# A post-norm attention and mixture-of-experts block on one core: reciprocals turned and spread by DMA, squares by one load, the output projection accumulated, and the swaps issued by ScalarE

## The reference

```python
# attention: 16 heads of 64, rotary embedding on interleaved pairs, causal
q, k, v = x @ Wq, x @ Wk, x @ Wv           # (128, 1024) each, split into heads
q, k = apply_rope(q), apply_rope(k)
attn = softmax(causal(q @ k.T / 8))
x = layernorm(x + (attn @ v) @ Wo + bo)
# mixture: 8 experts of 512, the best 2 of a softmax gate, renormalised
sparse_w = top2(softmax(x @ gate_w.T + expert_bias))
out = sum_e sparse_w[e] * (gelu(x @ w_up[e].T) @ w_down[e].T)
x = layernorm(x + layernorm(out) + x)      # the inner norm is the block's own
```

## Time and profile before

| | us |
|---|---|
| median of 3 runs | 805.34 |
| lowest and highest of them | 800.24, 806.1 |
| the profiled execution | 798.51 |
| its span, first to last instruction | 796.7 |

### The profile page before, as it was taken

How to read it: one execution, slowest core, us unless ns; L and a number is a source line. 1 busy time by engine, 2 the same in 40 slices (tenths; PEclk the granted TensorE clock), 3 DMA queues, 4 the chain that set the end, 5 groups by cost and what they waited for, 6 DMA issues and landing times.

```text
span 796.7 us, 20539 instructions
## 1 busy us (share of the span) xinstructions
PE 755.9 (95%) x5763; PEld 535.0 (67%) x5763; DVE 667.4 (84%) x2514; ACT 592.2 (74%) x1678; POOL 572.0 (72%) x701
## 2 busy tenths in 40 slices
PE   8899999999999999999999989999998899999995
PEld 4455666666666566666666656666656579999995
DVE  6688888999899879998999899989987974235997
ACT  3688878878878777877887768777877756565677
POOL 3686767558765877677768886976786266989983
PEclk9999999999999999999999999999999999999998
DMA  4576666456755566556555655565557667434525
GB/s 152 188 224 200 214 203 201 165 191 197 227 180 174 174 200 195 188 180 210 175 186 191 194 173 186 186 199 173 177 179 225 222 193 207 109 85 125 163 90 163
DMA packets 110719, 144.66 MB, mean 182 GB/s; under 512 B 13392, under 2 KB 86352, under 8 KB 110608
## 3 DMA queue, kind: packets, MB, share of 16 engines
q1 hardware_dynamic: 106240, 134.49, 53.8%
q0 software_dynamic: 4224, 8.72, 3.3%
q10 hardware_dynamic: 144, 0.13, 0.1%
HBM read 61.42 MB, written 45.17 MB: 134 GB/s over the span
## 4 chain that ended last, share of the span: by engine, by line
PE 67%; POOL 13%; DVE 8%; issue 7%; DMA 3%; ACT 1%; SPq 0%; DVEq 0%; POOLq 0%; ACTq 0%
PE AO L1109 15%; PE S_all L1068 14%; PE TB L1089 9%; PE AO L1129 5%; PE S_all L1256 4%; POOL yrows L956 4%; PE TB L1269 2%; POOL shared L973 2%; PE AO L1269 2%; DVE Sm L1609 2%; DMA qk<-shared 2%; DVE x_acc L1630 1%; PE TB L1000 1%; POOL shared L722 1%; PE TB L998 1%
## 5 line engine op out<-in xcount | busy, mean ns | idle before, releaser
L1376 ACT ACTIVATE Pr_all<-Sm,nmax 128x512 f32<-128x512 f32 (+3 forms) x512 | 281.8, 563 | 23.7 <-DVE nmax L1609 22.9
L1609 DVE CUSTOM_DVE_ANT_0 Sm<-S_all,causal 128x512 f32<-128x512 f32 (+3 forms) x512 | 223.0, 482 | 46.0 <-PE S_all L1068 45.9
L1068 PE MATMUL S_all<-qk 64*128 64x512 f32 (+3 forms) x1024 | 169.8, 446 | 10.9 <-DVE nmax L1609 8.6
L717 POOL TENSOR_TENSOR qk<-shared,qk 128x512 f32<-128x512 f32 x64 | 81.9, 1280 | 129.6 <-DMA qk<-shared 119.9
L1109 PE MATMUL AO<-PT,shared 128*64 128x128 f32 x1008 | 149.6, 438 | 13.1 <-issue 12.7
L1386 ACT ACTIVATE PT<-TB 128x768 f32<-128x768 f32 x189 | 107.8, 605 | 61.2 <-PE TB L1089 61.2
L1630 DVE SCALAR_TENSOR_TENSOR x_acc<-AO,rinv,x_acc 128x128 f32<-128x128 f32 x504 | 141.7, 344 | 3.5 <-POOL x_acc L769 1.3
L1068 PEld LDWEIGHTS S_all<-qk 64*128 64x128 f32 x1024 | 79.7, 187 | 82.6 <-issue 56.9
L1089 PE MATMUL TB<-ident,Pr_all 128*128 128x128 f32 x764 | 109.2, 279 | 3.6 <-ACT PT L1386 3.1
L1089 PEld LDWEIGHTS TB<-ident,Pr_all 128*128 128x128 f32 x764 | 82.0, 141 | 44.4 <-issue 40.6
L1109 PEld LDWEIGHTS AO<-PT,shared 128*64 128x64 f32 x1008 | 66.5, 136 | 61.1 <-issue 30.9
(11 more groups left out here) (335 smaller groups left out, 1459.0 us busy)
## 6 DMA issues: line engine op xcount, KB each, us to landing
turns<-turned_pr SPq DMA_DIRECT2D x63, 512.0 KB
PT<-turns SPq DMA_DIRECT2D x252, 128.0 KB
qk<-shared SPq DMA_DIRECT2D x124, 256.0 KB
wo<-in_wo SPq DMA_DIRECT2D x64, 64.0 KB, 3.1
PT<-yrows SPq DMA_DIRECT2D x7, 512.0 KB, 4.3
w_tile<-in_wup SPq DMA_DIRECT2D x10, 256.0 KB, 3.5
xt<-xrows SPq DMA_DIRECT2D x32, 65.0 KB, 2.7
x_acc<-in_x SPq DMA_DIRECT2D x8, 256.0 KB, 3.4
```

Of the source, the lines that this page charges most:

```text
L717: nc.gpsimd.tensor_tensor(qT[p][:, :], q_cos, qT[p][:, :], ALU.add).then_inc(q_ready, 1)
L1068: nc.tensor.matmul(SB[2 * (group % 2) + h][:, at:at + (qb + 1) * P], qT[p][half, qb * P:qb * P + P], kT[p][half, 0:(qb + 1) * P], start=Tr ...
L1376: nc.scalar.activation(Pr[j][:, 0:n], Sm[j], ACT.Exp, bias=nmax[:, j:j + 1], scale=-1.0, accum_out=rsum[p][:, h * QB + qb:h * QB + qb + 1] ...
L1609: nc.vector.tensor_tensor_reduce(out=Sm[j], in0=SB[2 * (group % 2) + h][:, at:at + n], in1=causal[:, T - n:T], scale=-0.125, scalar=HUGE, ...
```

## The change

1. **Reciprocals** (`invert`, `spread_norms`, `norm_o`): DVE inverts the row sums of unit u-1 at the head of iteration u and transposes them in squares of 32. SP writes them to a DRAM buffer `norms` (128 pieces of 128 bytes), waits for their landing, and reads them back spread over 128 partitions, 512 values in each, into a buffer: two rows of 2 KB, each repeated for 64 partitions. DVE multiplies the attention's output with them as it takes it from PSUM to OT (`norm_o`), in the place of ScalarE's `copy_o` and of DVE's `scale_y`, which stays for the last unit alone.
2. **Projection**: with OT already divided, `project_out` needs four products of 128 rows in the place of eight of 64, and accumulates over the 8 pairs of a sequence in one PSUM bank; DVE adds the bank to `x_acc` once a sequence (`add_y`). Wo is loaded in the first eight units and then kept.
3. **Squares by one load**: `store_turned` writes the rows in another order, so that one DMA of 512 KB can read back what four read before.
4. **Scores in one run**: group 2 has banks of its own (TB), and DVE masks all three groups without `scale_y` between them; the transposes of group 1 go to the score banks. `project_out` follows score group 2.
5. **Swaps**: ScalarE issues the two DMAs of `swap(u+1)`, between the last `exp` of unit u-1 and the first of unit u.

SP's order in an iteration is now: `spread_norms(u-1)` (store, wait, spread), `store_turned(u)`, wait, `load_turned(u)`.

```diff
-LOADED = LANES * 16
+LOADED = 16
...
+        def spread_of(u):
+
+            if u < PAIRS:
+                e = E - 2 + u % 2
+                return wdown[:, e * IB:e * IB + IB, :].rearrange("p a c -> p (a c)")
+            return hT[u % 2][:, :]
...
+        rinv, rinv_turned = (st2[:, i, :, :].rearrange("p n s -> p (n s)")[:, 0:SQ] for i in range(2))
...
-        def y_bank(u):
-            return (SB[2], SB[3]) if u == UNITS - 1 else (AB, OB)
+        y_bank, last_y = OB, (SB[2], SB[3])
 
         def turn_banks(u, group):
 
-            two = TB if u < UNITS - 1 or group == 0 else S_all[:, 2 * group - 2:2 * group, :]
+            two = S_all[:, 0:2, :] if group == 1 else S_all[:, 2:4, :] if group == 2 and u == UNITS - 1 else TB
             return two.rearrange("k b n -> k (b n)")
+
+        def score_bank(group, h):
+            return TB[:, h, :] if group == 2 else SB[2 * group + h]
+
+        def wo_of(u):
+
+            if u < PAIRS or u % PAIRS >= 6:
+                return wo[u % 2][:, :]
+            return w_tile[u % PAIRS // 4][:, u % 4 * P:u % 4 * P + P]
...
                 if first:
                     load_x(0)
+                elif u <= PAIRS:
+                    load_wo(u - 1)
+                if not first:
+                    spread_norms(u - 1, 1 - p)
+                if not last:
+                    store_turned(u, p)
+                    load_turned(u, p)
...
-                if not last:
-                    store_turned(u, p)
-                if first:
-                    load_turned(u, p)
...
+            def spread_norms(u, p):
+
+                sp.wait_ge(inverted, 2 * u + 2)
+                wait(sp, norms_in, 16 * (u - 1))
+                sp.dma_start(norms[p * SQ:p * SQ + SQ, :].rearrange("c (a r) -> a c r", r=SQ), rinv_turned).then_inc(norms_stored, 16)
+                sp.wait_ge(norms_stored, 16 * (u + 1))
+                wait(sp, norms_in, 16 * u)
+                wait(sp, o_ready, u - 1)
+                if u == PAIRS:
+                    sp.wait_ge(q_proj, PAIRS)
+                    sp.wait_ge(k_proj, PAIRS)
+                    sp.wait_ge(w_split, PAIRS // 2)
+                heads = norms[p * SQ:p * SQ + BLK, :].rearrange("(h q) t -> h (q t)", h=2)
+                sp.dma_start(spread_of(u), heads.unsqueeze(1).to_broadcast([2, D, T])).then_inc(norms_in, 16)
+
             def store_turned(u, p):
 
                 sp.wait_ge(turned, 2 * u + 2)
                 wait(sp, turns_in, LOADED * (u - 1))
-                sp.dma_start(turns[p * P:p * P + P, :], turned_pr[:, :, :, :].rearrange("p b c s -> p (b c s)")).then_inc(stored, 16)
+                sp.dma_start(turns[p * P:p * P + P, :].rearrange("(r a) n -> a r n", a=LANES),
+                             turned_pr[:, :, :, :].rearrange("p b c s -> p (b c s)")).then_inc(stored, 16)
 
             def load_turned(u, p):
 
                 sp.wait_ge(stored, 16 * (u + 1))
+                wait(sp, turns_in, LOADED * u)
                 wait(sp, pv_done, u - 1)
-                squares = turns[p * P:p * P + P, :].rearrange("(a r) (b n) -> b r a n", r=SQ, b=LANES)
-                for b in range(LANES):
-                    sp.dma_start(PT[p][SQ * b:SQ * b + SQ, LANES * (QB - 1):, :, :].rearrange("k a c s -> k a (c s)"),
-                                 squares[b]).then_inc(turns_in, 16)
-
-            def swap(u, p):
-
-                sp.wait_ge(k_read, u + 1)
-                sp.wait_ge(q_read, u + 1)
-                wait(sp, scored, BLK * (u - 1))
-                sp.dma_start(qk[p][0:P:2, :, :], qk_rot[1:P:2, :, :]).then_inc(swapped, 16)
-                sp.dma_start(qk[p][1:P:2, :, :], qk_rot[0:P:2, :, :]).then_inc(swapped, 16)
+                squares = turns[p * P:p * P + P, :].rearrange("(r a) (b n) -> b (r a) n", a=LANES, b=LANES)
+                sp.dma_start(PT[p][:, LANES * (QB - 1):, :, :].rearrange("k a c s -> k (a c s)"), squares).then_inc(turns_in, 16)
...
             def project_q(u, n, batch):
                 inputs_ready(n, batch)
-                if u == 2:
-                    pe.wait_ge(v_ready, 2)
-                elif u > 2:
-                    pe.wait_ge(pt_ready, 2 * (u - 3) + 1)
+                if u >= 2:
+                    pe.wait_ge(maxed, BLK * (u - 1))
...
             def transpose(u, p, group):
                 pe.wait_ge(exped, BLK * u + DONE_BY[group])
-                if u == UNITS - 1 and group > 0:
+                if u == UNITS - 1:
                     pe.wait_ge(maxed, BLK * UNITS)
+                    pe.wait_ge(pt_ready, 2 * u)
                 elif group == 2:
 
-                    pe.wait_ge(pt_ready, 2 * u + 1)
+                    pe.wait_ge(maxed, BLK * (u + 2))
                 else:
-                    wait(pe, pt_ready, 2 * u)
-                    pe.wait_ge(q_read, min(u + 3, UNITS))
-                    if u == 0:
-                        pe.wait_ge(k_read, 2)
+                    pe.wait_ge(maxed, BLK * (u + 1) + DONE_BY[0])
...
+                for i in range(QB):
+                    last = nc.tensor.matmul(y_bank[:, i * P:i * P + P], OT[p][:, i * P:i * P + P], wo_of(u),
+                                            start=(first and i == 0), stop=last_pair, skip_group_check=True)
+                last.then_inc(y_done, 1)
...
-                wait(pe, maxed, BLK * u)
+                wait(pe, maxed, BLK * (u - 1) + DONE_BY[1])
+                wait(pe, pt_ready, 2 * (u - 2) + 1)
                 score(u, p, 0)
-                if u >= 2:
...
+                    pe.wait_ge(maxed, BLK * u)
+                    wait(pe, pt_ready, 2 * (u - 1))
+                    pe.wait_ge(q_read, min(u + 2, UNITS))
                 score(u, p, 2)
+                if u >= 2:
+                    project_out(u - 2, p)
...
-                if u >= 2:
-                    copy_o(u - 2, p)
                 if not first:
                     for j in range(FIRST_OF[2], BLK):
                         exp(u - 1, 1 - p, j)
+                if 2 <= u < UNITS - 1:
+                    swap(u + 1, 1 - p)
...
+            def swap(u, p):
+
+                act.wait_ge(k_read, u + 1)
+                act.wait_ge(q_read, u + 1)
+                act.wait_ge(scored, BLK * (u - 1))
+                nc.scalar.dma_start(qk[p][0:P:2, :, :], qk_rot[1:P:2, :, :]).then_inc(swapped, 16)
+                nc.scalar.dma_start(qk[p][1:P:2, :, :], qk_rot[0:P:2, :, :]).then_inc(swapped, 16)
...
             def invert(u, p):
 
                 dve.wait_ge(exped, BLK * (u + 1))
-                wait(dve, y_read, 2 * u)
-                nc.vector.reciprocal(rinv[:, :], rsum[p][:, :]).then_inc(inverted, 1)
+                nc.vector.reciprocal(rinv[:, 0:BLK], rsum[p][:, :]).then_inc(inverted, 1)
+                if u < UNITS - 1:
+                    dve.wait_ge(inverted, 2 * u + 1)
+                    wait(dve, norms_stored, 16 * u)
+                    nc.vector.transpose(rinv_turned, rinv).then_inc(inverted, 1)
+
+            def norm_o(u, p):
+
+                dve.wait_ge(pv_done, u + 1)
+                dve.wait_ge(norms_in, 16 * (u + 1))
+                wait(dve, y_done, u - 1)
+                nc.vector.tensor_tensor(OT[p][:, :], o_bank(u), spread_of(u), ALU.mult).then_inc(o_ready, 1)
+
+            def add_y(b):
+
+                dve.wait_ge(y_done, min(PAIRS * (b + 1), UNITS - 1))
+                dve.wait_ge(x_set, b + 1)
+                rows = x_acc[:, b * QB:b * QB + QB, :].rearrange("p a c -> p (a c)")
+                nc.vector.tensor_tensor(rows, y_bank, rows, ALU.add).then_inc(y_read, 1)
...
+                if u >= 2:
+                    norm_o(u - 2, p)
+                if not first:
+                    invert(u - 1, 1 - p)
```

More of the change, by code:

```diff
@@ L22 @@
 BLK = 2 * QB
+Y_READS = B + 2
 ORDER = [(0, 3), (1, 3), (0, 2), (1, 2), (0, 0), (1, 0), (0, 1), (1, 1)]
@@ L142, with build_block @@
 HUGE = 3.0e38
-def build_block(nc, xT_h, x_h, wqk_h, wv_h, wo_h, bo_h, cos_h, sin_h, gate_h, ebias_h, wup_h, wdown_h, xrows, yrows, turns, out_h):
+def build_block(nc, xT_h, x_h, wqk_h, wv_h, wo_h, bo_h, cos_h, sin_h, gate_h, ebias_h, wup_h, wdown_h, xrows, yrows, turns, norms, out_h):
     ctx = ExitStack()
@@ L370, in build_block @@
         o_ready = sem("o_ready")
+        norms_stored, norms_in = sem("norms_stored"), sem("norms_in")
         y_done = sem("y_done")
@@ L400, in build_block @@
         y_in = [sem(f"y_in{i}") for i in range(B - 1)]
-        y_last_in = [sem(f"y_last_in{i}") for i in range(QB)]
+        y_last_in = [sem(f"y_last_in{i}") for i in range(len(PARTS))]
         summed, last_summed, spaced = sem("summed"), sem("last_summed"), sem("spaced")
@@ L545, in _, with load_wo, keep_wo @@
             rows, experts = [], []
+            def load_wo(u):
+                wait(sp, y_done, u - 1)
+                sp.dma_start(wo[u % 2][:, :], wo_h[bass.ds((u % PAIRS) * P, P), :]).then_inc(wo_in[u % 2], 16)
+            def keep_wo():
+                rows = wo_h.rearrange("(n p) c -> p n c", p=P)
```

(36 more changed lines are left out.)

105 lines of the change are left out of this document (54 added, 51 removed).

## The result

The changed kernel takes 1812.0 us (median of 4 runs, 1806.2 to 1817.8) against 803.1 us (4 runs, 800.2 to 806.1): 2.256 times the time before, 95% interval 2.243 to 2.269. The forecast was 1560 us, with a range up to 1800.

The account below looks back on a forecast made before the run. Few DMA engines on store, load and spread were to bound each unit through SP's chain, 22 us instead of 9.79; 62 x (22 - 9.79) = 757 us on 796.7, with 1.8 around it 1556, gave 1560 us, range 1240 to 1800.

Parts of the forecast that it names:

- The signs that the forecast named: DMA share below 0.5, two SP landing waits of 5 us or more, store at about 100 GB/s, stores 22 us apart.
- the sum of SP's chain: SP's queue per unit: spread 5.9, store 5.2, latency 1.3, load 6.6, small store 0.8, latency 1.3, issues 0.5: 21.6 us.
- load 131 / 19.8 = 6.6 us: Single load of the turned group: a quarter, 131 thousand bytes, per engine in 1 KB pieces, 6.6 us a unit.
- 5.9: Spread of the reciprocals: half of it on each of two engines in 2 KB pieces, 5.9 us a unit.
- 131 / 25.3 = 5.2 us: Store of the turned group: a quarter, 131 thousand bytes, per engine in 4 KB pieces, 5.2 us a unit.
- 26 us and 1800 us: Unit and kernel time if latencies double and swaps and small store fall fully into SP's chain.
- The waits between score group 2 and the masks go: Attention unit: these waits disappear, worth at most 0.6 us a unit.
- DVE's lighter unit: DVE loses eight instructions and gains a multiplication and a small transpose: 1.9 us less a unit.
- the first rival: All sixteen engines work on every transfer; units at 9.3 us, about 775 us, faster; chance 0.12.
- All sixteen engines: Every DMA transfer uses all sixteen engines, so PE runs closed up: about 775 us; chance 0.12.
- ACT holds the swap: Sixteen engines, but swaps wait for the last exp on ACT; POOL's loop 10.3 us, 830 us; chance 0.03.
- Only the spread is narrow: Other transfers re-cut over sixteen engines; SP's chain 12.4 us a unit, 960 us; chance 0.03.

Follow-up runs that it names:

- r_k8: o_wide_sp with the 64 repeats of each spread transfer's source written as 8 x 8 (outermost count 8): the spread moves for 2.6 us (median).
- r_k2: o_wide_sp with the 64 repeats of each spread transfer's source written as 2 x 32 (outermost count 2): the spread moves for 7.3 us (median).
- w_load: Changed kernel with only the load cut into four transfers of 32 partitions: 1443.0 us, a unit of 19.8.
- w_store: Changed kernel with only the store cut into four transfers of 32 rows, new row order kept: 1450.9 us, a unit of 19.9.
- b_one_load: Kernel before with only the store's new row order and the single load of 512 KB: 1237.8 us, a unit of 16.6.
- a_tiny: Changed kernel with swaps of 16 of the 512 columns: 1696.7 us, a unit of 23.7.
- w_spread: Changed kernel with only the spread cut into one transfer per head, outermost count 64: 1690.1 us, a unit of 23.7.
- n_sp: Changed kernel with old store and four loads, swaps issued by SP, small store and spread left out, norm_o multiplying by the cosine table: 795.8 us, ratio 0.986.
- o_wide: Changed kernel with the store and four loads of before, and the spread cut by heads into two transfers: 878.1 us, ratio 1.092.
- o_wide_sp: o_wide with SP issuing the swaps between the store and the loads, as before: 859.5 us, ratio 1.067.
- o_act: o_wide_sp with the small store and the spread issued by ScalarE at two places of its unit: 834.7 us, ratio 1.038.
- n_act: n_sp with the swaps issued by ScalarE: 811.5 us, ratio 1.005.
- o_squares: Changed kernel with the row order and four loads of before put back, the spread staying narrow: 1207.1 us, unit 16.1.

## Why the prediction was right in its mechanism and short in its size

**The mechanism held.** Transfers with outermost counts of 4, 4 and 2 run on that few engines: `r_k8` to `r_k2` show it for one dimension alone, `w_load`, `w_store` and `b_one_load` for the load and the store. The signs that the forecast named came: a DMA share of 0.28 with two grown waits of SP, DVE waiting 624.3 us for the spread, busy shares of PE and DVE near half and a third. Two came in another size: stores 25.7 us apart and not 22, and a store alone on its engines at 60 GB/s and not about 100. PE's lowered clock stayed beside the path, as said.

**The step that failed is the sum of SP's chain**, "21.6 us", taken as 22: it measured 25.67 us, and 62 x 3.67 = 227 us of the 250 that were missing in the profiled execution (1806.2 - 1556). By terms, from the means of the 63 units in SP's queue and the DMA records between its issues:

- Second half, load to landing of the small store: forecast 6.6 + 0.8 + 1.3 and half of the issues, 8.95 us; measured 12.1. The swaps on the same engines are 1.7 of the 3.1 missing (`a_tiny`); the forecast had "up to 1.3" for them and took 0.4. Another 1.0 goes with what no term stood for, other transfers that SP issues between the load and the small store: in the 31 units without them this half takes 11.1 us, in the 32 with them 13.1. The last 0.4 is in the terms themselves. The term "load 131 / 19.8 = 6.6 us" is a load that moves for 8.5 us in the median unit, and for 7.4 with the small swaps.
- First half, spread and store: forecast 12.65 us; measured 13.6. The term that was too small is the spread, "5.9", which moves for 7.0 us in the median unit. The store, forecast at "131 / 25.3 = 5.2 us", ends 5.0 us after it; the 8.4 us that it needs with four engines at once (`w_spread`) don't arise here. The other 1.6 us were forecast as 1.55.
- The tail had no term: from the last store to the end 192.5 us instead of 168.6, +24. The last unit's own narrow store and load lie there; its load could be issued 13.0 us after the store instead of 2.7.

25.67 us a unit with this tail gives 1556 + 227 + 24 = 1807 us. The range's upper end, "26 us and 1800 us", held the unit and missed the time by its missing tail.

**The gains.** "The waits between score group 2 and the masks go" and DVE's lighter unit: `n_sp` has 9.69 us a unit, 0.10 less than before, where the first rival had 9.3. They are a gain of 1.4%, not of 4%. Whether more was held back by POOL's loop of swaps (it waited 103.8 us there in `n_sp`, 119.9 before) wasn't tried.

**The rivals.** *All sixteen engines* is refuted by `r_k2`; its price was too low as well, since with all large transfers wide (`o_wide`) the kernel takes 878.1 us and not 775. The forecast saw the latencies of the reciprocals' way only as part of a narrow chain. They cost 64 us on their own: a ring of 9.1 us or more in SP's queue becomes the bound (`o_wide_sp`) or, with that queue relieved, the landing of the spread holds up a third of the units (`o_act`). *ACT holds the swap* names the right loop and the wrong cause: the swap isn't held, it lands 0.65 us later (`n_act` against `n_sp`). That is worth 15.7 us (forecast: some 30); behind the narrow transfers it wasn't to be seen. *Only the spread is narrow* was given as 960 us and is 1207.1 in `o_squares`: from the store to its landing took 10.0 us where the chain of 12.4 had 5.9 + 1.4 + 1.3 = 8.6, since the spread moved for 7.5 us, and the chain had no issues in it, 1.73 us for the loads alone.

**What stays open.** Why pieces of 4 KB take 224 ns on average when four engines store at once, and 159 when the last two do, with gaps besides. What the accumulated projection and the scores in one run are each worth, since `n_sp` has both.

## What to carry to other kernels

Before merging transfers, write down the outermost count of both sides of the merged one, after every rearrangement and broadcast: at 2, 4 and 8 the smaller one was also the number of engines here, and fewer issues can cost far more than they save (605 us here, with a row order that only served to merge them). The mean DMA share hides this; a low share together with long waits for landings is the sign. A small way through DRAM and back holds an in-order queue for its latency even with wide transfers (412.22 - 408.55 = 3.7 us a unit in `o_wide_sp`, of a unit of 9.8), so it belongs on a queue that has that much to spare; and for a transfer that closes a tight loop the queue that issues it is worth a measurement: the same swaps cost 16 to 19 us more from ScalarE's.

## What the runs showed of the hardware that was not expected

A store of 512 KB on four engines moved at 60 GB/s, 15 for each engine that its count allows, where an engine moved 25 GB/s in pieces of the same size before. The issue of a store in the new row order takes 533 ns (median) where the plain one took 338. And an issue behind a load on few engines stretches: the small store, 16 KB, takes 1.5 us to issue (median) and up to 3.7, but 0.55 and at most 1.0 in `w_load`, where the load is wide. The first line is of the kernel after, the second of `w_load`.

```profile
L586 SPq DMA_DIRECT2D norms<-st x63: 503/1465/3712, 34.5 to 1627.7; - x63
L586 SPq DMA_DIRECT2D norms<-st x63: 543/551/973, 36.1 to 1269.3; - x63
```
